# A ring of four PSUM banks, exponentials in place, every fourth product on GpSimd, and small transfers spread between the wide ones

## The reference

```
dt_in, Bs, Cs = (xp[..., :DTR], xp[..., DTR:DTR + N], xp[..., DTR + N:])
delta = jax.nn.softplus(dt_in @ w_dt + b_dt)
A = -jnp.exp(A_log)
def step(h, t):
    dt, bt, ct, xt = t
    h = jnp.exp(dt[:, :, None] * A) * h + (dt * xt)[:, :, None] * bt[:, None, :]
    return (h, jnp.einsum('bdn,bn->bd', h, ct))
```

## Time and profile before

| | |
|---|---|
| median of 3 runs | 1220.89 us (1219.04 to 1223.19) |
| profiled execution | 1217.73 us |
| its span | 1215.9 us |
| granted clock of PE, mean | 0.842 |
| DVE busy | 1074.0 us, 88% of the span |
| PE, ACT, POOL busy | 902.4, 809.6, 815.2 us |
| DMA queue of SP | 47.6% of the 16 engines' time |

### The profile page before, as it was taken

How to read it: one execution, slowest core, us unless ns; L and a number is a source line. 1 busy time by engine, 2 the same in 40 slices (tenths; PEclk the granted TensorE clock), 3 DMA queues, 4 the chain that set the end, 5 groups by cost and what they waited for, 6 DMA issues and landing times. The chain is left out here.

```text
span 1215.9 us, 19663 instructions
## 1 busy us (share of the span) xinstructions
PE 902.4 (74%) x4292; PEld 366.9 (30%) x4292; DVE 1074.0 (88%) x2434; ACT 809.6 (67%) x2199; POOL 815.2 (67%) x558
## 2 busy tenths in 40 slices
PE   4276778787788766887678776777778776787875
PEld 1022332333333232332223333233233322333332
DVE  4389989989899988999899998899989998999993
ACT  4277764878648765577657876477864877656772
POOL 6466765867567766677667676586766777667663
PEclk9558988879887888879888898788988888897887
DMA  4544356543584344644456335553358434574440
GB/s 118 124 130 122 117 132 144 151 113 91 132 200 127 117 112 118 169 130 117 114 139 157 114 119 130 146 144 117 90 133 200 127 117 104 128 181 138 119 117 9
DMA packets 124123, 155.29 MB, mean 128 GB/s; under 512 B 32722, under 2 KB 57062, under 8 KB 124006
## 3 DMA queue, kind: packets, MB, share of 16 engines
q1 hardware_dynamic: 123494, 153.74, 47.6%
q0 software_dynamic: 512, 0.27, 0.2%
HBM read 137.63 MB, written 4.52 MB: 117 GB/s over the span
## 5 line engine op out<-in xcount | busy, mean ns | idle before, releaser
L1338 POOL TENSOR_TENSOR prod<-hst,C 128x1024 f32<-128x1024 f32 x256 | 603.4, 2357 | 340.5 <-DVE hst L1151 340.5
L1151 DVE TENSOR_TENSOR_SCAN hst<-bank,dbx 128x512 f32<-128x512 f32 x512 | 618.8, 1210 | 35.4 <-ACT bank L626 35.4
L626 ACT ACTIVATE bank<-wide,A_rep 128x512 f32<-128x512 f32 x512 | 351.6, 687 | 319.7 <-DVE hst L1151 221.7
L1145 DVE TENSOR_TENSOR dbx<-bank,B 128x512 f32<-128x512 f32 x512 | 342.7, 670 | 56.0 <-PE bank L871 46.4
L871 PE MATMUL bank<-spread,sel_bc 96*128 96x512 bf16 x512 | 218.1, 441 | 66.3 <-DVE dbx L1145 47.0
L640 ACT ACTIVATE prob<-s_sb,nmax 128x96 f32<-128x96 f32 x512 | 183.9, 360 | 0.0
L892 PE MATMUL bank<-prod,sel_red 128*32 128x512 f32 x1024 | 164.1, 718 | 4.3 <-POOL prod L1338 4.3
L902 PE MATMUL bank<-k,q 128*128 128x384 f32 x256 | 137.8, 626 | 30.4 <-DVE nmax L1164 19.1
L909 PE MATMUL bank<-ident,prob 128*96 128x128 f32 x512 | 92.2, 311 | 61.9 <-ACT ao L656 61.6
L871 PEld LDWEIGHTS bank<-spread,sel_bc 96*128 96x128 bf16 x512 | 55.0, 108 | 219.9 <-DVE dbx L1145 146.5
L1343 POOL TENSOR_TENSOR prob<-prob,pinv 128x384 f32<-128x384 f32 x128 | 106.1, 829 | 8.8 <-DVE pinv L1172 6.3
(11 more groups left out here) (180 smaller groups left out, 926.5 us busy)
## 6 DMA issues: line engine op xcount, KB each, us to landing
wide<-dt_rows SPq DMA_DIRECT2D x512, 256.0 KB, 4.5
vw<-v_tok SPq DMA_DIRECT2D x80, 64.0 KB, 3.0
spread<-parts SPq DMA_DIRECT2D x96, 32.0 KB, 1.9
x_sb<-in_L_attn_x_dram SPq DMA_DIRECT2D x8, 256.0 KB, 4.6
dt_rows<-sp_t SPq DMA_DIRECT2D x8, 256.0 KB, 4.5
out_dram<-outb SPq DMA_DIRECT2D x8, 256.0 KB, 2.2
q<-qn SPq DMA_DIRECT2D x112, 16.0 KB
vw<-v_tok SPq DMA_DIRECT2D x16, 48.0 KB, 2.6
```

The lines of the kernel that those rows point to most:

```text
L626: nc.scalar.activation(daP[s % 2][:, :], wide[m % SLOTS][:, s % 2, :], ACT.Exp, scale=A_rep[:, g:g + 1]).then_inc(exp_done, 1)
L1145: v.tensor_tensor(dbx[:, s % 3, :], uP[s % 2][:, :], B2[p][:, :], ALU.mult).then_inc(dbx_done, 1)
L1151: v.tensor_tensor_scan(hst[:, s % 4, :], daP[s % 2][:, :], dbx[:, s % 3, :], 0.0, ALU.mult, ALU.add).then_inc(scan_done, 1)
L1338: g.tensor_tensor(prod[:, 2 * (m % 4):2 * (m % 4) + 2, :], hst[:, 2 * (m % 2):2 * (m % 2) + 2, :], C2[p][:, :].unsqueeze(1).to_broadcast([ ...
```

## The change

Five things are changed together.

1. One ring of four banks (uP[0..3], bank q for the units with s mod 4 = q) takes the place of two banks for exp and two for u. For q = 0, 1, 2 the matmul of u writes the bank, DVE multiplies with B in place in it, and the scan reads it; `dbx` is gone. exp is computed in place in the wide tile in SBUF. PE and ACT work three units ahead instead of one (U_AHEAD, AHEAD).
2. For q = 3 there is no matmul of u and no product on DVE. u is written to DRAM (u_rows), brought back by DMA into `uwide`, repeated 64 times, two units a tile (widen_u), and POOL multiplies it with B in place (pool_input), in the slots with s mod 4 = 1. The exponential of these units goes to bank 3.
3. unit_u now waits for the scan of unit s - 4 (wait value s - 3), not for a product; PE's slot s therefore begins when scans up to s - 1 are done, except at s mod 4 = 0, where there is no matmul of u.
4. widen waits for the scans of pair m, not for its exponentials.
5. SP's small transfers are taken apart: parts at m = 18, 21, 23 (nine instead of twelve), heads four each at m = 26, 27, 28, 29, keys at m = 30, values two each at m = 0 to 5 of the batch that uses them, and two DMAs of widen_u at every m with m mod 4 = 3.

```diff
-ROWS_AT = {"store": 10, "rows": 16, "parts": 19, "heads": 26, "keys": 28, "values": 31}
+ROWS_AT = {"store": 10, "rows": 16}
+PART_DMA_AT = {18: 0, 21: 1, 23: 2}
+HEAD_DMA_AT = {26: 0, 27: 1, 28: 2, 29: 3}
+KEY_DMA_AT = 30
+VALUE_DMA_AT = {0: (0, 0), 1: (0, 2), 2: (1, 0), 3: (1, 2), 4: (2, 0), 5: (2, 2)}
...
-AHEAD = 1
+AHEAD, U_AHEAD = 3, 3
...
-        daP, uP, yP, sP, ptP, jobP = bank[0:2], bank[2:4], bank[4], bank[5], bank[6], bank[7]
+        uP, yP, sP, ptP, jobP = bank[0:4], bank[4], bank[5], bank[6], bank[7]
...
+            def widen_u(B, p, m):
+
+                wait(sp, scan_done, B * UNITS + 8 * (m - U_SLOTS) + 8)
+                if m == 0:
+                    wait(sp, urows_out, (B + 1) * 16)
+                flat = u_rows.rearrange("a d t -> (a d t)")
+                for j in range(2):
+                    row = p * 32 + 4 * m + j
+                    src = bass.AP(flat.tensor, flat.offset + row * L, [[0, 64], [2 * L, 2], [1, L]])
+                    sp.dma_start(uwide[m % U_SLOTS][64 * j:64 * j + 64, :, :], src).then_inc(uwide_in[m % U_SLOTS], 16)
+
             def widen(B, p, m):
 
-                wait(sp, exp_done, B * UNITS + 2 * (m - SLOTS) + 2)
+                wait(sp, scan_done, B * UNITS + 2 * (m - SLOTS) + 2)
...
+                    if m % 4 == 3:
+                        if m // 4 + U_SLOTS < GROUPS // 2:
+                            widen_u(B, p, m // 4 + U_SLOTS)
...
+                    if m in VALUE_DMA_AT and not first(B):
+                        window_values(B, *VALUE_DMA_AT[m])
...
+                        if m in HEAD_DMA_AT:
+                            spread_heads(sp, B + 1, HEAD_DMA_AT[m])
+                        if m == KEY_DMA_AT:
                             keys(B + 1)
...
-                wait(act, scan_done, B * UNITS + s - 1)
                 g = GROUPS * q + i
-                nc.scalar.activation(daP[s % 2][:, :], wide[m % SLOTS][:, s % 2, :], ACT.Exp,
+                to = wide[m % SLOTS][:, s % 2, :]
+                if q == POOL_Q:
+                    wait(act, scan_done, B * UNITS + s - 3)
+                    to = uP[q][:, :]
+                nc.scalar.activation(to, wide[m % SLOTS][:, s % 2, :], ACT.Exp,
...
-                wait(pe, dbx_done, B * UNITS + s - 1)
-                mm(uP[s % 2][:, :], sel_bc[:, i, :, :].rearrange("k j n -> k (j n)"), spread[p][:, q, :],
+                wait(pe, scan_done, B * UNITS + s - 3)
+                mm(uP[q][:, :], sel_bc[:, i, :, :].rearrange("k j n -> k (j n)"), spread[p][:, q, :],
...
-                v.tensor_tensor(dbx[:, s % 3, :], uP[s % 2][:, :], B2[p][:, :], ALU.mult).then_inc(dbx_done, 1)
+                i, q = divmod(s, 4)
+                if q == POOL_Q:
+                    return
+                wait(dve, u_ready, B * POOL_Q * GROUPS + POOL_Q * i + q + 1)
+                v.tensor_tensor(uP[s % 4][:, :], uP[s % 4][:, :], B2[p][:, :], ALU.mult).then_inc(dbx_done, 1)
...
-                v.tensor_tensor_scan(hst[:, s % 4, :], daP[s % 2][:, :], dbx[:, s % 3, :], 0.0, ALU.mult,
+                v.tensor_tensor_scan(hst[:, s % 4, :], decay[:, :], into[:, :], 0.0, ALU.mult,
...
+            def pool_input(B, p, i):
+
+                if i == 0:
+                    wait(pool, done["p"], job_count("p", B, "B"))
+                if i % 2 == 0:
+                    wait(pool, uwide_in[(i // 2) % U_SLOTS], (B * (GROUPS // 2 // U_SLOTS) + i // 2 // U_SLOTS + 1) * 32)
+                u = uwide[(i // 2) % U_SLOTS][:, i % 2, :]
+                g.tensor_tensor(u, u, B2[p][:, :], ALU.mult).then_inc(gbx_done, 1)
...
+                    if s % 4 == 1:
+                        if s // 4 + 1 < GROUPS:
+                            pool_input(B, p, s // 4 + 1)
```

More of the change, by code:

```diff
@@ L94 @@
 SLOTS = 4
+U_SLOTS = 2
+POOL_Q = 3
 UNIT_PAIRS = UNITS // 2
-N_PARTS_DMA = 12
+N_PARTS_DMA = 9
 SP = {n: i + 1 for i, n in enumerate(
@@ L205, in hybrid_block_kernel @@
         vw = sb("vw", [3 * W, NBLK, KVH, 32])
-        dbx = sb("dbx", [128, 3, L])
         hst = sb("hst", [128, 4, L])
@@ L259, in hybrid_block_kernel @@
         wide_in = [sem(f"wide_in{c}") for c in range(SLOTS)]
+        urows_out, gbx_done = sem("urows_out"), sem("gbx_done")
+        uwide_in = [sem(f"uwide_in{c}") for c in range(U_SLOTS)]
         q0_in, q_in = sem("q0_in"), sem("q_in")
@@ L308, in hybrid_block_kernel, with spread_heads @@
         N_FIRST_DMA, N_W_DMA = 13, 18
-        def spread_heads(eng, B):
+        def spread_heads(eng, B, g):
             wait(eng, done["p"], job_count("p", B, "q"))
[L314 to L319, removed]
+            for r in range(REP):
+                h = g * REP + r
+                eng.dma_start(q4[32 * g:32 * g + HD, :, r, :],
+                              qn[h * HD:(h + 1) * HD, :].rearrange("p (n q) -> p n q", q=W)) \
+                    .then_inc(q0_in if first(B) else q_in, 16)
         def wait_heads(eng, B):
@@ L414, in body @@
                             store_rows(B + 1, 1 - p)
[L415 to L419, removed]
+                        if m in PART_DMA_AT:
+                            spread_parts(B + 1, 1 - p, PART_DMA_AT[m])
+                        if m in HEAD_DMA_AT:
+                            spread_heads(sp, B + 1, HEAD_DMA_AT[m])
+                        if m == KEY_DMA_AT:
                             keys(B + 1)
-                        if m == ROWS_AT["values"]:
-                            window_values(B + 1)
             def load_weights():
@@ L443, in load_weights, with spread_parts @@
                 assert n == N_W_DMA
[L445 to L451, removed]
+            def spread_parts(B, p, part):
+                wait(sp, sp_step, B * N_SP + SP[("hi", "mid", "lo")[part]])
+                for c in range(POOL_Q):
+                    sp.dma_start(spread[p][32 * part:32 * part + 32, c, :],
+                                 parts[32 * c:32 * c + 32, part, :]).then_inc(parts_in, 16)
             def keys(B):
@@ L878, in front @@
                     pre_job(name, B, p, front=True)
-                unit_u(B, p, 0)
+                for s in range(U_AHEAD):
+                    unit_u(B, p, s)
             def y_start(B, p):
@@ L1330, in front @@
                 other_constants()
-                spread_heads(pool, B)
+                for i in range(KVH):
+                    spread_heads(pool, B, i)
+                pool_input(B, p, 0)
             def pair_product(B, p, m):
@@ L1356, in body @@
                         pair_product(B, p, s // 2)
+                    if s % 4 == 1:
+                        if s // 4 + 1 < GROUPS:
+                            pool_input(B, p, s // 4 + 1)
+                        elif not last(B):
+                            pool_input(B + 1, 1 - p, 0)
                     k = block_at(s, NORM_LAG)
```

50 lines of the change are left out of this document (32 added, 18 removed).

## The result

The changed kernel takes 1302.28 us (median of four runs, 1300.57 to 1302.91) against 1220.54 for the kernel before (four runs, 1219.04 to 1223.19): 1.066 times as long, 95% interval 1.063 to 1.068. It missed by 96 us. The profiled execution has a span of 1298.7 us.

A forecast was written before the change was run, and what follows sets the result against it. DVE, busy 88% of the span, was taken as the bound. Batches 1 to 6 at -1.3 us each (-8), batch 7 +6.2 and batch 0 -13 gave -15 on 1217.7: 1203, or 1206 for the median; range 1145 to 1235.

The forecast's parts named there:

- Term 1: 16 slots a batch without a product on DVE save 0.58 us each: 9.3 us a batch, 74 us in all.
- Term 2: DVE's waits for exp and mid-batch u go: 9.7 us a middle batch, 8 in batch 0, 2.2 in batch 7.
- Term 3: Keys land after the batch's last scan: DVE waits 7.5 us at slot 2, plus 0.9, in batches 1 to 7.
- Term 4: The last value windows land late, PE is held in slot 12: DVE waits 4.6 us in batches 1 to 7.
- Term 5: POOL, with its added products, is level with DVE; its extra steps make DVE wait 3.0 us a batch.
- PSUM as target: DVE's product u*B written to a PSUM bank: bounds -8 to +22 us over 384 products, taken as 0.
- The rival that rested on it: DVE's product into a bank costs more: gain gone at +40 ns, 1228 us at ACT's +56; chance 0.17.
- Term 6: PE's slot begins later, as unit_u waits for scan s - 1, delaying scores for DVE: 1.7 us a batch.

The follow-up runs named there:

- the run with all three: Changed kernel with keys issued from ACT's queue, value windows four each at m = 0 to 2, and U_AHEAD 2: 1157.42 us, ratio 0.950.
- The added work: Changed kernel plus four small zero-matrix matmuls on TensorE in slots 18, 19, 22 and 23 of every batch: 1278.91 us, ratio 1.047.
- the run with the product back on DVE: The run with all three, but DVE instead of GpSimd makes the product u*B of every fourth unit, in the same SBUF tile: 1217.65 us, ratio 0.998.

## Why the prediction was wrong

- **Term 1 (products off DVE)** held as busy time: two scans side by side are 1.13 us apart in batch 3 (556.58 and 557.71), and the run with all three has DVE busy 994.4 us, the kernel before with its parts apart 1070.7, 76 less where 74 was forecast (some 10 of them are the tensor_scalar of the last section, against 4 more in `cs`). As time it is worth less: these two runs are 1157 and 1189, 29 apart by their ratios (40 in the profiled executions, where DVE idles 37 us more).
- **Term 2 (waits removed)** held: waits for exp fell from 35.4 to 3.6. By itself the half of it that lies in SP's order is worth 33 us in the kernel before.
- **Term 3 (keys too late)** held at 6.9 to 8.9 us where 7.5 was forecast. But only 25 us of it come back when the keys are early and TensorE's slot is not.
- **Term 4 (value windows too late)** held, 5.5 to 6.1 for 4.6, though its own parts add up to 6.7, not "near 7.0"; in time they give 35 us.
- **Term 5 (POOL)** was too large: 0.5 us a batch against 3.0 (its own count gave 2.0), and 2.0 in the run with all three.
- **PSUM as target** costs nothing that the cadence shows: from scan to scan with a product between it is 1.71 us as before; the product itself lasts 685 ns against 670, 6 us of busy time in all. The rival that rested on it is out. Its +56 ns from ACT was misread: the earlier trace rows compares a tanh, whose scale is a constant, with exp, whose scale is read from a tile. Exp against exp, the changed kernel has 713 ns in SBUF and 682 into a bank, so ACT's rows show no dearer bank either.
- **Term 6 (PE begins its slot later) is the step that failed**: 1.7 us a batch forecast, 11.0 measured in batch 3 (six blocks of scores 8.9, three memory scores 2.1). The mechanism was named rightly, its size was not, for two reasons. "2.0 in all" for u, reduction and scores, and the 0.81 of the earlier trace rows, are times at the full clock (granted clock 1.00 around that row); the trace has 4.1 at half clock. The other row, 1.49 us at a clock of 0.50, was at hand, and term 3 used it. And only three blocks were charged, where six are late. The step never asked what TensorE does until the scan is done: it idles, 246.6 us in all, and the lower clock follows. A lead of two gives 74 us back. The added work shows that the clock alone costs 23 us at two of the six blocks.

The ledger of batch 3, forecast 143.5 - 1.3 = 142.2 and measured 151.5, so 9.3 too long: term 6 +9.3 (11.0 for 1.7); DVE's busy time +1.9 (124.7 for 132.1 - 9.3), which no term had; term 4 +1.4; term 3 -1.1 (7.3 for 8.4); term 5 -2.5. Together +9.0; the rest is other small waits. Of DVE's 1.9 the product is 0.7 (48 x 15 ns), the tensor_scalar of the last section 0.5 and `cs` 0.2.

The rule of the Trainium skill (TensorE: Matmul & The Clock Gate, HAM oscillation — how this bites in real kernels) says that idle gaps between bursts of matmuls bring the lower clock back, which then slows the next burst; its example is a wait for DMA. The rows agree in this, with a wait for DVE: 0.50 behind 2.17 us of idle time, 1.00 in the same place with the gaps filled.

In short: SP's order gains 33 us, GpSimd's products with the ring of banks 29 on top of it, and three choices (the lead of u, where the keys are issued, where the value windows are issued) lose 142. The losses were not needed for the gains: without them the kernel, with the keys on ACT's queue, is 5% faster than before.

What stays open: how the 74 us of the lead divide between the clock, the earlier start and some 10 us of the instruction that met GpSimd; what the ring of banks gives by itself, since no run has it without the transfers of u; and whether exp in place in SBUF (713 ns for 682 into a bank) costs time, which no run varied.

## What to carry to other kernels

A longer lead is not free when the engine that runs ahead waits for a later event to free its buffer: what stands behind that wait in its program order is delayed by the same amount. Price a job on TensorE behind a wait at the lower clock, not at that of its best row, and look for filler or an earlier start before moving work elsewhere. When transfers are spread out in time, count back from the first reader of each, with everything that the queue must issue before it.

## What the runs showed of the hardware that was not expected

Some DVE instructions with all operands in SBUF take turns with GpSimd. In batch 3 of the changed kernel a tensor_scalar on DVE starts 0.01 us behind a product on GpSimd and takes 2.62 us; in the run with a lead of two it starts 0.20 us ahead of one, takes 0.53, and the product takes 2.53 instead of 2.35:

```profile
589.76 2.62 DVE L1152 TENSOR_SCALAR sp_t<-xn 128x512 f32<-128x512 f32 x1
```
```profile
589.75 2.35 POOL L1382 TENSOR_TENSOR prod<-hst,C 128x1024 f32<-128x1024 f32 x1
```
```profile
558.88 0.53 DVE L1152 TENSOR_SCALAR sp_t<-xn 128x512 f32<-128x512 f32 x1
```
```profile
559.08 2.53 POOL L1382 TENSOR_TENSOR prod<-hst,C 128x1024 f32<-128x1024 f32 x1
```

The Trainium skill (SBUF — State Buffer, Who interferes with whom) describes this as an exclusive lock that the first comer holds for its whole instruction; these rows agree.

So does the product with both inputs in SBUF, in the run with the product back on DVE. Here it starts 0.53 us behind a product on GpSimd:

```profile
577.17 2.39 DVE L1181 TENSOR_TENSOR uwide<-uwide,B 128x512 f32<-128x512 f32 x1
```
```profile
576.64 2.37 POOL L1384 TENSOR_TENSOR prod<-hst,C 128x1024 f32<-128x1024 f32 x1 [1.04 <-DVE hst L1196]
```

`cs`, a product of two SBUF tiles, is a third: 0.66 us in the kernel before, 0.88 to 4.14 in the changed kernel, where GpSimd is at work beside it each time. Not all do: the statistics of the layer norm, with all operands in SBUF, take at most 0.30 us, whether GpSimd is at work beside them or not. Nor is any of it seen in the products and scans with one operand in a bank (in the changed kernel the longest of 384 products takes 0.70 us and the longest of 512 scans 1.22). That fits how little GpSimd's extra 166 us beside them cost.
